# Front of a tile reordered, a loop edge behind the third down block, and column loads issued later, in a fused attention and feed-forward kernel

## What is computed

```python
qkv = x @ w_qkv.T                       # q, k, v: 16 heads of 32
q = q * cos + rotate_half(q) * sin      # k likewise
scores = where(keep, einsum('bhqd,bhkd->bhqk', q, k) * scale, -inf)   # 0 <= row - col < 64
x = layernorm(x + (softmax(scores) @ v) @ w_out.T)
gate = silu((x @ w_gate) * s_gate); up = (x @ w_up) * s_up
x = layernorm(x + ((gate * up) @ w_down) * s_down)
```

## Time and profile before

| | us |
|---|---|
| median of 3 runs | 1166.68 |
| lowest, highest | 1164.76, 1167.25 |
| the profiled execution, device time | 1166.12 |
| its span (first to last instruction) | 1164.3 |
| PE busy | 1148.5 (99%) |
| DVE, ACT, POOL busy | 976.0, 622.3, 600.5 |
| granted TensorE clock, mean | 0.998 |

### The profile page before, as it was taken

How to read it: one execution, slowest core, us unless ns; L and a number is a source line. 1 busy time by engine, 2 the same in 40 slices (tenths; PEclk the granted TensorE clock), 3 DMA queues, 4 the chain that set the end, 5 groups by cost and what they waited for, 6 DMA issues and landing times.

```text
span 1164.3 us, 25889 instructions
## 1 busy us (share of the span) xinstructions
PE 1148.5 (99%) x8577; PEld 595.0 (51%) x8577; DVE 976.0 (84%) x2797; ACT 622.3 (53%) x1724; POOL 600.5 (52%) x570
## 2 busy tenths in 40 slices
PE   9999999999999999999999999999999999999998
PEld 4344446464464644646455464554645545464444
DVE  7889998889997899878999789887898978986434
ACT  3863883159920689117980279702796038950330
POOL 0775684356731667326771367614676245752330
PEclk9999999999999999999999999999999999999999
DMA  9999786357672585717757077561874627644000
GB/s 295 161 186 242 140 172 147 85 100 139 121 174 56 96 139 112 175 40 124 138 98 166 37 142 127 97 160 38 151 123 91 166 58 136 126 74 109 19 1 37
DMA packets 353042, 139.59 MB, mean 120 GB/s; under 512 B 309968, under 2 KB 332624, under 8 KB 352912
## 3 DMA queue, kind: packets, MB, share of 16 engines
q1 hardware_dynamic: 334976, 106.86, 49.6%
q0 software_dynamic: 10800, 18.09, 5.3%
q10 hardware_dynamic: 7136, 12.93, 3.2%
HBM read 36.13 MB, written 9.18 MB: 39 GB/s over the span
## 4 chain that ended last, share of the span: by engine, by line
PE 78%; DVE 7%; issue 6%; POOL 3%; DMA 3%; ACT 2%; SPq 1%; ACTq 0%; DVEq 0%; POOLq 0%
PE bank L906 52%; PE bank L1217 17%; PE bank L916 3%; PE bank L1143 2%; DMA xT_sb<-xT_sb 2%; DVE v_own L1794 2%; POOL xT_sb L690 1%; ACT bank L1457 1%; PE bank L1123 1%; ACT fuse L1356 1%; POOL fuse L695 1%; DVE ffn_tmp L1844 1%; DMA qkT<-fuse 1%; DVE bank L1831 1%; DVE probs L1809 1%
## 5 line engine op out<-in xcount | busy, mean ns | idle before, releaser
L906 PE MATMUL bank<-x1T,wg 128*128 128x512 f16 (+1 forms) x1032 | 242.5, 378 | 1.1 <-DVE ffn_tmp L1844 1.1
L906 PE MATMUL bank<-x1T,wu 128*128 128x512 f16 x1024 | 241.9, 379 | 0.0
L1457 ACT ACTIVATE bank<-bank,neg_max,qk_scale 128x128 f32<-128x128 f32 x512 | 220.4, 434 | 23.5 <-DVE neg_max L1837 22.4
L1217 PE MATMUL bank<-wd,fuse 128*128 128x512 f16 (+2 forms) x1056 | 223.3, 373 | 0.7 <-DVE y L1892 0.6
L695 POOL TENSOR_TENSOR fuse<-ffn_tmp,fuse 128x512 f16<-128x512 f32 x128 | 149.7, 1170 | 96.5 <-ACT fuse L1356 96.2
L800 POOL TENSOR_TENSOR fuse<-fuse 128x512 f16<-128x512 f32 x116 | 142.6, 1266 | 88.3 <-ACT fuse L1356 86.1
L1217 PEld LDWEIGHTS bank<-wd,fuse 128*128 128x128 f16 x1056 | 101.6, 98 | 118.7 <-DVE y L1892 1.6
L906 PEld LDWEIGHTS bank<-x1T,wu 128*128 128x128 f16 x1024 | 100.2, 98 | 120.6
L690 POOL TENSOR_TENSOR xT_sb<-probs,xT_sb 128x512 f16<-128x512 f32 x112 | 131.0, 1170 | 52.2 <-ACT xT_sb L1356 52.0
L906 PEld LDWEIGHTS bank<-x1T,wg 128*128 128x128 f16 x1032 | 96.4, 98 | 112.7 <-DVE ffn_tmp L1844 2.0
L1366 ACT ACTIVATE ffn_tmp<-bank,tanh_scale 128x512 f32<-128x512 f32 x128 | 88.7, 693 | 65.9 <-PE bank L906 42.2
(11 more groups left out here) (258 smaller groups left out, 1846.7 us busy)
## 6 DMA issues: line engine op xcount, KB each, us to landing
v_cross<-v_own SPq DMA_DIRECT2D x64, 128.0 KB, 2.4
out<-x ACTq DMA_DIRECT2D x31, 256.0 KB, 2.0
xT_sb<-xT SPq DMA_DIRECT2D x30, 256.0 KB, 4.9
qkT<-x SPq DMA_DIRECT2D x28, 256.0 KB, 3.2
wg<-w_gate POOLq DMA_DIRECT2D x7, 1024.0 KB, 5.7
v_cross<-kept_v_weights ACTq DMA_DIRECT2D x5, 768.0 KB, 7.5
wu<-w_up POOLq DMA_DIRECT2D x7, 512.0 KB, 6.3
wqkv<-w_qkvT SPq DMA_DIRECT2D x8, 256.0 KB, 6.2
```

The lines of the kernel that those rows point to most:

```text
L906: last = pe.matmul(dst, lhsT, rhs, start=(i == 0 and not onto), stop=(i == len(pairs) - 1), skip_group_check=onto)
L1217: last = pe.matmul(dst[:, cols], fuse[:, s, z, rows], wd[:, s, cols], start=(s == 0 and z == 0), stop=(s == STEPS - 1 and z == 1))
L1457: last = act.activation(unit, unit, ACT.Exp, bias=neg_max[:, s % 2, h // 3, h % 3:h % 3 + 1], scale=qk_scale[:, 2:3], accum_out=row_sum[:, ...
```

## The change

Four things are changed; the number of instructions that do arithmetic stays the same on each engine.

1. In `project_values` `values_second(a, 0)` moves up four places and the two `scores` move up four products, so that they follow `values_seventh(a, 0)`. ACT moves `exponentials(a, 0)` and `(a, 1)` and the copies of the values ahead of most of the rounding of queries and keys: only the first half of `split_high(a, 2)` stays early. DVE takes the maxima of both score groups before it completes value block 1, and `weights(a, 0)` and `weights(a, 1)` come earlier among `add_v` and `split_v`; `weights(a, 0)` gets a new wait for `values_seventh(a, 1)`, since it overwrites what that product reads.
2. On PE `spread_maximum` and `down(f, 2)` move from `back` to the end of `front`. The sequence of products is the same; the back edge of the loop now lies between down blocks 2 and 3.
3. On POOL `reload_columns` moves from behind the second `invert_deviation1` to behind the last row copy, ahead of `split_low(a + 1, 0)`. In tile 7 it stays.
4. Indices of `v_product` follow the new order.

```diff
-        V_FIRST, V_FIFTH, V_SIXTH, V_THIRD, V_SEVENTH, V_SECOND, V_FOURTH = range(7)
+        V_FIRST, V_FIFTH, V_SIXTH, V_THIRD, V_FOURTH = 0, 1, 2, 3, 6
+        V_SECOND, V_SEVENTH = (4, 5), (5, 4)
...
                     for j in range(NB):
                         invert_deviation1(a, j)
-                        if j == 1:
+                        if j == 1 and not more:
                             reload_columns(a)
...
                 if more:
+                    reload_columns(a)
                     split_low(a + 1, 0, ffn)
...
             def project_values(a):
                 values_sixth(a, 0)
                 values_third(a, 0)
+                values_second(a, 0)
                 values_fifth(a, 1)
                 values_seventh(a, 0)
+                scores(a, 0, True)
+                scores(a, 1, True)
                 values_sixth(a, 1)
-                values_second(a, 0)
                 values_fourth(a, 0)
                 values_third(a, 1)
                 values_seventh(a, 1)
-                scores(a, 0, True)
-                scores(a, 1, True)
                 values_second(a, 1)
                 values_fourth(a, 1)
...
-                for j in range(2):
+                for j in range(NB - 1):
                     down(f, j, attn)
+                    if more and j == 1:
+                        spread_maximum(a)
 
             def back(t, more, attn=True):
                 a, f = t, t - 1
-                if more:
-                    spread_maximum(a)
-                for j in range(2, NB):
-                    down(f, j, attn)
+                down(f, NB - 1, attn)
...
                     keep_values_seventh(a, 0)
+                    split_high(a, 2, ffn, range(2))
                     keep_values_sixth(a, 1)
-                    split_high(a, 2, ffn)
+                    exponentials(a, 0, ffn)
                     keep_values_seventh(a, 1)
-                    split_high(a, 3, ffn)
-                    exponentials(a, 0, ffn)
                     keep_v(a, 0, ffn)
                     keep_v(a, 1, ffn)
+                    split_high(a, 2, ffn, range(2, 4))
                     exponentials(a, 1, ffn)
+                    split_high(a, 3, ffn)
                     keep_v(a, 2, ffn)
                     keep_v(a, NB - 1, ffn)
...
                     add_v(a, 0)
-                    add_v(a, 1)
                     for s in range(2):
                         maxima(a, s, ffn)
                         bias(a, s)
-                        add_v(a, 2 + s)
+                    add_v(a, 1)
+                    wait(v_product[1], dve, a - 2, V_SEVENTH[1])
                     weights(a, 0, ffn)
-                    for j in range(2):
-                        split_v(a, j, ffn)
+                    add_v(a, 2)
+                    split_v(a, 0, ffn)
+                    add_v(a, NB - 1)
+                    split_v(a, 1, ffn)
                     weights(a, 1, ffn)
```

More of the change, by code:

```diff
@@ L1408, in keep_values_seventh @@
             def keep_values_seventh(a, i):
-                keep_value_product(a, i, v_rows(2 * i + 1)[:, 0:HALF_EMB], v_places(i)[3], V_SEVENTH)
+                keep_value_product(a, i, v_rows(2 * i + 1)[:, 0:HALF_EMB], v_places(i)[3], V_SEVENTH[i])
             def carry_v(a):
@@ L1786, in add_v @@
                 wait(v_products_kept[i], dve, a - 2, 2 + back)
-                wait(v_product[i], dve, a - 2, V_FOURTH if back else V_SECOND)
+                wait(v_product[i], dve, a - 2, V_FOURTH if back else V_SECOND[i])
                 done(v_added, dve.scalar_tensor_tensor(out=v_rows(j), in0=bank32[j], scalar=v_scale[:, 1:2],
```

## The result

The changed kernel takes 1184.4 us (median of 1183.8 to 1189.7), the kernel before beside it 1165.9: a ratio of 1.017, with a 95% interval of 1.014 to 1.020. I had forecast 1172.5, within 1161.5 to 1177.5: the sign was right, the size wrong by 12 us, and the time lies outside the range.

A forecast was written before the change was run, and what follows sets the result against it. PE, busy 99% of the span, was taken as the bound. Span 1164.3 + 7.7 (six fronts) − 1.5 (column loads and edge) = 1170.5, execution 1172.3, forecast 1172.5 us, range 1161.5 to 1177.5.

The forecast's parts named there:

- The back edge: PE's four taken loop branches: the same four waits return in the new place, 0 instead of up to −1.2 us.
- The front: PE at `weigh_v` 1 waits 2.3 us for transposed probabilities; net +1.3 us in each of six, +7.7 us.
- ACT's 4.1 us: ACT's second half of block 2 ends at 545.6 instead of 541.5, 4.1 us later, in tile 4.
- SP's back-to-back issues: SP's queue from block 2's transposes on: no idle left, probabilities 1 issued at 558.75 instead of 556.93.
- the credit of 6.1: PE's existing waits in six fronts, 6.1 us, mean 1.02, taken as swallowed by the new `weigh_v` 1 wait.
- is no term of its own: DVE's late gate bank read, PE's gate product waiting 1.5 instead of 0.2 us: unpriced, as PE waits for `weigh_v` 1 anyway.
- DVE's contention: `split_v` 2 and 3 fall into POOL's last four subtractions; if both take 1.64 us, the gate product waits 1.5.
- rival C: Gate product of step 2, not transposes: about +1.1 us a front, 1172; shares slower's 0.61, of which the forecast has 0.45.
- The column loads: Loads moved on POOL behind the last row copy: DVE's wait in tile 5 goes, −0.9 to −1.6 us.
- The clock: PE's granted clock is 1.00 in every stretch of the loop, upper level 2.4 GHz throughout; no term given.
- A: Transposes land in time at `weigh_v` 1, wait 0.4 us: faster, 1159, or 1163 with half the contention; chance 0.24.
- B: Gains and losses balance: a wait of 1.0 to 1.6 us at `weigh_v` 1, 1164.5 to 1169; chance 0.15.

The follow-up runs named there:

- the loads alone: Kernel before with only the column loads moved behind the last deviation, except in tile 7: 1164.1 us, ratio 0.9988.
- the front alone: Kernel before with only the reordering of values, scores, exponentials and weights and its indices; loop edge and column loads unchanged: 1176.4 us, ratio 1.0096.

## Why the prediction was wrong

- **The back edge: the step that failed.** "The loop still branches once a tile" led to a term between 0 and −1.2; it is +9.9. I took the four waits of the kernel before (0.1, 0, 0.3, 0.8) as the price of a taken branch wherever it stands. They were the price at one position: in the kernel before the loop's target stands 33 matmuls earlier, the next late place lies some 36 matmuls behind it, nearly 8 us, and PE's instructions are there 2.6 to 3.6 us behind the branch, so it is fully covered. The order of PE ahead of the prediction shows the 32 products and the spread that moved ahead of the branch, and the Trainium skill's rule was in the text ("Runtime: NRT & Kernel Launch", "Instruction fetch mechanics"). What I did not do is count where in a block the target then stands. My bounds came from the rows of the same edge, and no row of the kernel before could have shown the other end: this term needed a range up to about +12, and the range's upper end should have said that. The front and the loads alone, +11.1 and −1.2, would have come to some 1176, inside my range.
- **The front: mechanism right, size low.** I expected a wait of 2.3 us at `weigh_v` 1 with SP's queue as cause; it is 1.5 to 2.2 in the loop's tiles, in the changed kernel and with the front alone. The 2.2 is tile 4, from whose rows I took it for all six. ACT's 4.1 us, POOL, SP's back-to-back issues: point by point, with 0.5 to 0.9 us more delay at SP than worked out. The net is 11.1, not 7.7. With the front alone the waits for the transposes total 11.0 where my 6 × 2.3 has 13.8. What was too large is the credit of 6.1 that I took off for the waits they would swallow: 2.0 of it were transposes of later groups and did go, but the gate product of step 2 stands ahead of `weigh_v` 1 and cannot be swallowed by it. It went from 0.2 to 0.5. This also sets right what I wrote of DVE, that its delay "is no term of its own": it is one of 2.0 us.
- **DVE's contention, half of it.** One `split_v` of the two pays 1.64, not both, hence 0.5 of wait and not 1.5; rival C had the place right and its price too high. The kernel before could have told: there too POOL was subtracting beside two of them, and the one ahead of 548.36 took 0.77. The Trainium skill, "SBUF — State Buffer", section "Who interferes with whom", has the second to start block. The trace agrees that the two hinder each other (1.64 against 0.68 alone, and POOL's subtractions beside it 1.6 instead of 1.16), but not that each pays for the other's whole instruction: the first of the pair also starts within a subtraction and loses only 0.1.
- **The column loads** were to give −0.9 to −1.6 and gave −1.2. Nothing was held up by them.
- **The clock** was in no term. I had written that PE runs at its upper level throughout, which held for the kernel before. Waits of 2 us bring stretches at 0.50 to 0.57 behind some of them, 1.7 us a time, over 5 us in the profiled execution.
- Rivals A and B fell. A needed waits below 1.0 at `weigh_v` 1, and no tile has one that short in total. B needed 1.0 to 1.6 and a time of 1164.5 to 1169; the loop's tiles have 1.5 to 2.2, and the front alone is at 1176.4.

## What to carry to other kernels

Work that moves across a loop's branch also moves the branch's target in the program, and so does every instruction added ahead of the loop: if a few equal waits for "issue" stand a fixed number of instructions behind each taken branch, shift the loop by some matmuls (here, eight fewer in the warm-up) before judging the change itself, because here 8 to 15 us came and went with unused instructions. When a result on a looped kernel surprises, compare it with a padded copy first. In a chain through several queues, ask which wait stands ahead of the new one in program order: only those behind it are swallowed.

## What the runs showed of the hardware that I had not expected

- The wait behind a taken branch goes by position: 2.3 to 3.0 us at three matmuls behind it, 1.6 to 2.3 at four, 0.95 to 1.33 at seven, at most 0.5 at twelve, none that shows with the target moved past the late place, and again 1.6 to 2.3 at four with 128 matmuls more ahead of the loop.
- What is late are the instructions themselves, and the trace has their transfers: packets of 16 KB on the queue named instruction. One starts 2.2 to 3.5 us ahead of each taken branch, and the products right behind the branch run without a stop; the next starts only 0.2 to 1.3 us behind the branch, and a product that needs it starts 1.3 to 1.6 us after its end.
- A wait of 2 to 3 us is followed in some cases, not in all, by 3 us or so at the lower clock (0.50, 0.51, 0.57), with no other cause to be seen. The runs do not say which waits are spared.
- Of two VectorE instructions beside GpSimd's subtractions, both with two inputs in SBUF, only one pays: 0.77 to 0.80 and 1.64, in three kernels, against 0.68 alone.
